# A selective scan whose ring of decays goes from three slots (two in PSUM, one in SBUF) to two, both in PSUM

## The reference

```python
delta = softplus(dt @ dt_proj_w.T + dt_proj_b)
deltaA = exp(delta[..., None] * A)                    # the decays
deltaBu = delta[..., None] * Bm[:, :, None, :] * xc[..., None]
h = dA * h + dBu                                      # along the 224 positions
y = einsum('bdn,bn->bd', h, c)
```

## Time and profile before

| what | us |
|---|---|
| median of 3 runs | 3315.78 |
| lowest and highest of them | 3312.24, 3319.89 |
| span of the profiled execution | 3316.6 |
| busy in it: PE, DVE, ACT, POOL | 2744.6, 2714.3, 1798.4, 1625.1 |
| first scan of batch 0 | starts at 85.28 |
| scan 0 of step 6, scan 0 of step 8 | 991.28, 1303.25 |
| last slots of the last batch | about 2530 |

### The profile page before, as it was taken

One profiled execution on the slowest core, in us unless ns is written; L12 is line 12 of the kernel. 1 busy time (PEld: TensorE's weight loads), 2 busy tenths in 40 slices (PEclk: granted clock), 3 DMA queues, 4 the chain that ended last, 5 costly groups with the idle time before them and its releaser, 6 DMA issues.

```text
span 3316.6 us, 37616 instructions
## 1 busy us (share of the span) xinstructions
PE 2744.6 (83%) x11840; PEld 2204.1 (66%) x11840; DVE 2714.3 (82%) x2657; ACT 1798.4 (54%) x3846; POOL 1625.1 (49%) x868
## 2 busy tenths in 40 slices
PE   4677978888787878787888788887877799999998
PEld 4566665757566666566666657576655588888886
DVE  6999999999999998999899999999997344444442
ACT  3566757565656666566657575656563333333331
POOL 1766666666666666665666665766663000000000
PEclk8899999999998999999999999999988799999999
DMA  8120202020120102020202020210202233333330
GB/s 285 41 62 6 68 12 73 7 73 29 50 63 17 65 15 65 14 73 6 74 12 67 12 73 10 69 50 24 65 9 102 83 123 118 110 111 118 120 124 17
DMA packets 90362, 208.65 MB, mean 63 GB/s; under 512 B 7684, under 2 KB 16516, under 8 KB 89415
## 3 DMA queue, kind: packets, MB, share of 16 engines
q1 hardware_dynamic: 80934, 184.45, 16.9%
q0 software_dynamic: 5120, 14.21, 1.4%
q10 hardware_dynamic: 4096, 7.34, 0.7%
HBM read 176.53 MB, written 29.98 MB: 62 GB/s over the span
## 4 chain that ended last, share of the span: by engine, by line
DVE 27%; PE 26%; issue 26%; POOL 16%; ACT 2%; DMA 2%; POOLq 0%; DVEq 0%; SPq 0%; ACTq 0%
POOL arena L800 12%; DVE ring L1047 10%; PE ring L1333 10%; PE work L1333 9%; DVE ring_sb L1047 7%; DVE arena L904 2%; PE y L1319 2%; DVE arena L1049 2%; PE work L1151 2%; POOL arena L747 1%; DMA arena<-bc_rows 1%; POOL arena L749 1%; PE work L1291 1%; DVE arena L875 1%; POOL arena L744 1%
## 5 line engine op out<-in xcount | busy, mean ns | idle before, releaser
L800 POOL TENSOR_TENSOR arena<-arena 128x896 f32<-128x896 f32 x512 | 1163.2, 2278 | 852.5 <-PE y L1319 837.4
L1319 PE MATMUL y<-arena,cst_sb 128*128 128x224 f32 x4096 | 992.1, 390 | 416.6 <-DVE arena L1049 415.5
L1319 PEld LDWEIGHTS y<-arena,cst_sb 128*128 128x128 f32 x4096 | 818.3, 207 | 569.9 <-DVE arena L1049 518.8
L1047 DVE TENSOR_TENSOR_SCAN ring<-ring,arena 128x896 f32<-128x896 f32 x352 | 711.5, 2021 | 31.3 <-POOL arena L800 25.3
L676 ACT ACTIVATE ring<-arena,small 128x224 f32<-128x224 f32 x1408 | 544.9, 436 | 277.3 <-DVE arena L1049 266.6
L1151 PE MATMUL work<-arena 128*128 128x224 f32 x2048 | 461.8, 372 | 38.8 <-DVE arena L904 27.4
L1047 DVE TENSOR_TENSOR_SCAN ring_sb<-ring_sb,arena 128x896 f32<-128x896 f32 x160 | 422.7, 2642 | 47.7 <-ACT ring_sb L676 47.5
L1151 PEld LDWEIGHTS work<-arena 128*128 128x128 f32 x2048 | 406.2, 202 | 64.4 <-DVE arena L904 31.4
L1102 DVE SCALAR_TENSOR_TENSOR hidden_lo<-work,hidden_hi 128x448 fp32r<-128x448 f32 x128 | 80.0, 625 | 387.9 <-ACT hidden_hi L714 387.9
L1049 DVE TENSOR_TENSOR arena<-ring,arena 128x896 f32<-128x896 f32 x352 | 384.2, 1091 | 12.0
L813 POOL DMA_INDIRECT out<-res,ids x32 | 42.7, 1336 | 670.6 <-DVE mst L1087 645.7
(11 more groups left out here) (146 smaller groups left out, 3719.2 us busy)
## 6 DMA issues: line engine op xcount, KB each, us to landing
weights<-in_w SPq DMA_DIRECT2D x64, 1024.0 KB, 6.9
arena<-bc_rows SPq DMA_DIRECT2D x128, 448.0 KB, 4.4
arena<-in_ctx SPq DMA_DIRECT2D x16, 896.0 KB, 5.7
expert_rows<-x2e SPq DMA_DIRECT2D x1, 7224.0 KB, 27.1
xrow<-expert_rows SPq DMA_DIRECT2D x8, 903.0 KB, 10.6
arena<-in_xT SPq DMA_DIRECT2D x16, 448.0 KB, 3.5
arena<-in_x SPq DMA_DIRECT2D x16, 448.0 KB, 3.5
out<-arena ACTq DMA_DIRECT2D x32, 224.0 KB, 2.3
```

Of the source, the lines that this page charges most:

```text
L800: nc.gpsimd.tensor_tensor(u[:, s % 4], dx[:, k:k + 1, :].to_broadcast([P, QN, L]), bc[:, 0, q * QN:(q + 1) * QN, :], ALU.mult).then_inc(u_ ...
L1047: nc.vector.tensor_tensor_scan(h, h, u_flat[:, s % 4, :], 0.0, ALU.mult, ALU.add).then_inc(scan_done, 1)
L1319: last = nc.tensor.matmul(o, ident, u[:, s % 4, i, :], start=False, stop=(q == Q - 1 and i == QN - 1))
```

## The change

The SBUF tile `ring_sb` and its place in the ring are taken out. Slot s uses tile s mod 2, in PSUM always. ACT may write the decays of slot s when the product of slot s - 2 is done, for every s. No instruction is added, moved or resized, on any engine; the operands of ten scans, ten products and forty exponentials of a step change from `ring_sb` to `ring`, the two PSUM tiles change their slots, and the wait ahead of the decays asks for one product more in slots 2 to 31.

```diff
-        ring_sb = sb("ring_sb", [P, SUB])
...
-        decays = [ring[:, 0, 0:SUB], ring[:, 1, 0:SUB], ring_sb[:]]
+        decays = [ring[:, 0, 0:SUB], ring[:, 1, 0:SUB]]
...
                     k, q = s // Q, s % Q
-                    back = 3 if s >= 2 else 2
-                    need(act, p_ready, b * SLOTS + (s + 1 - back))
+                    need(act, p_ready, b * SLOTS + (s + 1 - 2))
                     if s % (2 * Q) == 0:
                         act.wait_ge(delta_done, b * 4 + (s // (2 * Q) + 1))
                     for i in range(QN):
                         n = k * NS + q * QN + i
-                        last = nc.scalar.activation(decays[s % 3][:, i * L:(i + 1) * L], delta[:, k, :], ACT.Exp,
+                        last = nc.scalar.activation(decays[s % 2][:, i * L:(i + 1) * L], delta[:, k, :], ACT.Exp,
                                                     scale=a_neg[:, n:n + 1])
...
-                    h = decays[s % 3]
+                    h = decays[s % 2]
```

## The result

| | us |
|---|---|
| before, median of 4 runs beside it | 3314.46 (3312.24 to 3319.89) |
| with two PSUM tiles, median of 4 runs | 3345.46 (3340.63 to 3356.42) |
| ratio | 1.0089, 95% interval 1.0064 to 1.0114 |
| predicted | 3321, range 3275 to 3360 |

What follows compares the result with a forecast made beforehand. DVE's scan chain was taken to bound a step of 156.0 us; 12.4 us won against 12.7 of new waits makes a step 0.3 longer, 5 us over fifteen steps: 3321 us, range 3275 to 3360.

Steps and rivals of the forecast that it cites:

- its case: Prediction's own count: a step 0.3 us longer, time 3321; within 0.2% of 3315.8 counted as the same, 25% chance.
- What is won: DVE's scans and products in ten slots leaving SBUF: 15.4 us a step, 12.4 left after the stretch to scan 26.
- Slot 4: ACT's decay 4, side work 4 and decay 5 outlast DVE's slots 3 and 4: scan 5 waits 4.0 us.
- Slot 13: DVE's conv waits for decay 15 and the tap behind it on ACT: 2.5 us.
- Slots 11, 12 and 29: ACT's side work 11, 13 and 29 each within 0.6 us of DVE: waits of 1.4 us together, bounds 0 to 3.
- Slot 8: Decays 8 and 9 with ACT's side work outlast DVE: scan 9 comes 19.2 us after scan 6, a 4.8 us wait.
- The third rival: Slower through PE: lower clock after idling in the new waits delays its jobs for ACT; 3 us a step, 3366, 21%.
- From product 22 to scan 26: A chain through PE and ACT, not using the ring, keeps its length; DVE waits 5.7 us in place of 2.8.
- Slots 15 and 19: Within slots 14 to 21, where ACT's side work is short and DVE's long: nothing late, no wait counted.
- The number of steps: Fifteen steps have nearly all the side work: 15 x 0.3 = 5 us, from -42 to +51.
- The second rival: Faster in part: DVE's side work after waits at slots 4 and 8 meets POOL less; 3 us a step, 3272, 17%.
- The first rival: Faster, the whole gain: the lead isn't needed, a step 12.4 to 15.4 us shorter, 3131 us or less, 4%.

Runs made afterwards that it cites:

- the spread layout: ACT's side work spread over other slots, one table load more: on the changed kernel (two tiles) 3098.58 us, on the kernel before (three tiles) 3275.50 us.
- depth alone: Kernel before with its three tiles, one in SBUF, but ACT waits for product s - 2 in every slot: 3530.81 us.
- the two small moves: Changed kernel with, on ACT, the convolution's silu one slot earlier (3330.13 us), or the copy of t1 ahead of that of z0 (3333.8 us).
- the fastest kernel: Changed kernel with ACT's side work spread, and two small token operations moved from DVE to ACT: 3086.48 us.

## Why the prediction was right, and where it was off

The time is in the range, and the side is that of the largest chance, slower (0.41). The forecast itself was 24 us too low, and its case said no change that can be told; the result is one that can. That it is in the range is in part luck. The sum had fifteen steps alike, each longer by 0.3 us; steps 2 to 13 are longer by 3.4 each, at the very end of its bounds, and fifteen such steps would be 3366 us, outside the range. Steps 0 and 1, which won 11.2 and 6.9 us, brought it back.

- **What is won** was right: 12.4 us a step net, against 11.8 between the two rings with the spread layout and 11.0 between depth alone and the changed kernel. In the trace before, the excess of SBUF scans and products over 2.02 and 1.09 is 15.5 us a step in steps 2 to 13, where the sum took 15.4.
- **Slot 4**: a wait of 4.0 forecast, 3.88 in the row above, and 3.7 more than before on average. That it is side work 4 was shown by moving it.
- **Slot 13**: 2.5 forecast; 2.7 in nine of the twelve steps and 4 or more in the other three, 3.1 on average. **Slots 11, 12 and 29**: 1.4 forecast; 0.5, 0.3 and 0.8.
- **Slot 8** is the term that was mis-sized: 4.8 us of wait, that is 19.2 from scan 6 to scan 9, and it was 22.2 in the step shown and 22.0 on average. The count took ACT's rows as they were in the trace, without asking what ACT's later start does to PE. dt2's bank, freed later, held PE, PE restarted at half of 2.4 GHz, dt3 came 1.7 us late, and the correction took 1.0 more, beside one of POOL's products. The third rival had half of it: it named PE's lower clock after a pause, and dt3. It did not name the bank that made the pause.
- **From product 22 to scan 26**, the chain keeps its length only as long as its banks come in time: the copy that frees t1's stands behind decay 23, and so behind the ring. The stretch is 0.9 longer. DVE waits in it 1.85 + 4.76 = 6.6 us, where the prediction had 5.7.
- **Slots 15 and 19** have no term in the sum and are 1.0 us longer each, by small DVE operations that wait out POOL's products. On the other side, those of slots 5, 12 and 27 take 0.5, 1.75 and 0.4 us less than before, since they meet POOL less.
- **In sum**, over steps 2 to 13 and against the prediction's terms: 2.8 for slot 8, 0.8 for the stretch to scan 26, 2.0 for slots 15 and 19, 0.6 for slot 13, less 0.3 for slot 4, 0.5 for slot 5, 1.5 for slots 11, 12 and 29 together, and 0.6 for slots 0 and 27. That is 3.3 us a step, against the 3.1 by which the step was off.
- **The number of steps** was off as well, in the other direction, as said above.
- **The second rival**, that DVE's side operations behind a wait meet POOL less, holds in part: in slot 8 of the step shown the first of them (L875 before, L873 now) goes from 2.32 to 0.55 us, but the wait for the second hides it. All side operations of a step together are 1.0 us shorter, 35.3 to 34.3, and not 3.
- **The first rival**, 3131 us or less, was right of the ring and wrong of this kernel: it is what two tiles give once ACT's side work is spread (3098.58).

Left open: why slots 13, 15 and 19 are long in some steps of an execution and not in others, and how much of the times of the two small moves is due to it.

## What to carry to other kernels

The depth of a ring pays for long pieces of other work that its producer does between two items. Before adding or giving up a slot, list for each piece what the consumer does meanwhile. In this kernel, pieces under one item's length (3.06 us) plus the consumer's own side work cost little in a ring of two (DVE's waits for ACT in the scan fell from 351 us to some 130), and of a longer one the part over that shows, once per round. Spreading the pieces was worth more (247 us) than the third tile (212 between depth alone and before), and it let the faster memory win its 177. And when an engine starts later, follow the buffers that it frees too, not only the results that it gives.

## What the runs showed of the hardware

- A DVE operation on two elements a row took 3.42 us on average, and up to 4.04, beside POOL products on SBUF that ran one behind the other; it took 0.17 us in every step of the spread kernel. The prediction took this collision to be of the large SBUF scan, whose product had a mean of 2.08 us against 1.09.
- Scan and product with the ring tile in PSUM kept 2.01 to 2.03 and 1.09 us in all twelve kernels, whatever POOL did.
- After a pause of 7.61 us PE did four matmuls in 3.76 us, in place of 1.88: half of 2.4 GHz. The mean granted clock went from 0.935 before to 0.919 with the new waits, to 0.907 with depth alone, and to 0.963 in the fastest kernel: it was lower the more the other engines waited.
